# A table built one step earlier, scores on three banks and more filler products in a perceiver block

## The chip, the cores and the metric

The kernel runs on one core of a Trainium2 chip. TensorE (PE) multiplies, VectorE (DVE) and ScalarE (ACT) work elementwise and reduce, GpSimd (POOL) converts and issues some DMAs, SyncE (SP) issues the others. The metric is the device time of one execution in microseconds (us), the median of three runs. TensorE runs at one of two clock levels, 1.2 or 2.4 GHz; the profile gives the granted clock as a share of the higher.

## The reference

Six layers work on the tokens x, 8 x 32 tokens of width 256, each as x = x + f(layernorm(x)):

```python
x = x + L0_xattn(_layernorm(x), ctx)      # self and cross attention, projections rounded to fp8
x = x + L0_attn(_layernorm(x))            # causal conv, state-space scan
x = x + L0_ffn(_layernorm(x))             # 8 experts, the best 2 of each token
x = x + L1_xattn(_layernorm(x), ctx, mask)  # masked read of the contexts
x = x + L1_attn(_layernorm(x))            # rotary attention, 16 heads
x = x + L1_ffn(_layernorm(x))             # weights w = lut[idx], 16 values
```

The first is the longest. For each of 8 contexts of 512 rows it forms keys and values from the context, normalises each key, takes scores of 16 heads, a softmax, and mixes the values:

```python
kvx = einsum('bsi,oi->bso', cond, w_kv_x)
kx, vx = split(kvx, 2, axis=-1)
kx = _ln(kx.reshape(b, sc, g, d), kxln_w, kxln_b)
xout = _gqa(qx, kx, vx.reshape(b, sc, g, d))
core = _gqa(q, k, v)                      # the self attention, "core"
catq = _div_clamp_fp8(concatenate([core, xout]), proj_smooth)
return einsum('bsi,oi->bso', catq, wproj) * (proj_in_scale * proj_w_scale)
```

The last layer's weights are looked up: an index from 0 to 15 for each of 3 x 1536 x 128 elements, and a table of 16 values.

## The kernel before

**Front, to about 130 us.** PE centres a weight (L1511), then makes six projections of the tokens (`project`, L1438) and turns their heads (`turn`, L1456); DVE and ACT normalise the heads between. `cross_queries` (L1465, L1470) folds the keys' weight into the queries, which gives A and beta. The self attention is `scores_core` (L1487), a softmax on DVE and ACT, and `mix_core` (L1504), in two rounds. `z_act` is a semaphore by which DVE waits after each round of heads until ACT has its share done. The array beta is turned by four DVE transposes (L1780) between the two rounds of weights.

**Loop, steps b = 0 to 7, about 130 to 376 us.** Each engine has its own order of work, written out; semaphores join them. In step b PE does the scores of context b (four tiles t, each six products, `product`, L410 to L412), the mixing of context b-1 in two halves (L437) with the turning of the maxima (L420) and the softmax's sum (`total`, L446) between and behind them, the spread of the maxima (L427), in odd steps from 3 on the values of a pair of contexts (L488), and the keys of context b+1 (again L410 to L412, eight half tiles of six products each on banks 0 and 1). ACT splits A (L526), takes the inverse of the sums (L581, L582), splits the next context in two parts (L532), squares the keys with a sum (L543), takes the root (L553, L554) and the exponentials (L576). DVE scales the scores out of the bank (L663) and adds up the sum (L668), takes the maxima (L729 to L731), shifts (L736), normalises (L742 to L749) and makes the keys' scales (L710 to L714). The bank is chosen by

```python
                    if not (isinstance(b, int) and n < 2):
                        pe.wait_ge(scaled, n - 1)
                    product(bank(2 + t % 2), k, t, A_hi, lo).then_inc(st_full, 1)
```

**The table.** lut[idx] is a sum over 8 pairs of table values. For pair k and part m (of three) ACT makes a `leaf` (L618: one of the pair's two values, by the lowest bit of the index), DVE a `term` (L625: the leaf where the rest of the index is 2k, else 0), and a DMA of POOL's queue adds it to the table (L644). The leaf of pair k+1 and part m overwrites the term of pair k, so it waits for that DMA. Step b, from 1 to 6, does pair b-1; pairs 6 and 7 are done during the experts, each added by DVE (L635). The lowest bits are taken by DVE (L784, L785) after step 0.

**Tail, 376 us to the end.** The other five layers follow one another; each begins with a norm in DVE and ACT, after which PE turns h (L945). While PE has nothing to do it issues `keep_clock(n, bank)` (L937), n bf16 products of 128x512 with no use: 12, 14, 14, 14 and 14 of them ahead of the five norms' turning and 28 in the rotary attention.

## Time and profile before

| | us |
|---|---|
| median of 3 runs | 521.88 (520.35 to 522.84) |
| the profiled execution, its time | 520.56 |
| its span, first to last instruction | 518.7 |
| PE busy | 453.6 |
| DVE busy | 362.8 |
| ACT busy | 253.2 |
| mean granted clock | 0.967 |

The span lies 1.9 us below the profiled execution's time. Of the stages the front takes 130 us with PE busy for 103.12, the loop 246 with PE busy for 230.42, the experts (404 to 447) 43 with PE busy for 42.95, and the last three layers (447 to 518) 71 with 57.68. A row of the timeline has its start, its duration, the engine, the line and the operation, and in brackets the idle time ahead of it with what ended that. Neighbouring instructions of one line are put together, with their count after the x.

### The profile page before, as it was taken

The numbers are of one execution on the slowest core, as the hardware profiler recorded it, in microseconds if no ns is written. First come the engines' busy times: TensorE is split into PE (matmuls) and PEld (weight loads), VectorE is DVE, ScalarE is ACT, GpSimd is POOL, SyncE is SP. The second block draws the span as 40 slices with busy tenths as digits, with TensorE's granted clock in tenths as the row PEclk, the third lists the DMA queues.
The fourth block names the chain that finished last, engine by engine and source line by source line (L and its number), as shares of the span: only waits on it lengthen the run. The fifth ranks groups of instructions, "written<-read, shape, count | busy, mean of one in ns | idle before, by whom it ended". The sixth has DMA issues, their size and how long they took to land.

```text
span 518.7 us, 6469 instructions
## 1 busy us (share of the span) xinstructions
PE 453.6 (87%) x2222; PEld 307.4 (59%) x2228; DVE 362.8 (70%) x728; ACT 253.2 (49%) x790; POOL 21.9 (4%) x30
## 2 busy tenths in 40 slices
PE   1969897869999899899989999999667999788787
PEld 0434443457768475658656675657544888436466
DVE  5784848895594868589885888596765699734631
ACT  1366888674462675847766575842002343120110
POOL 0000000004000000100010010100020000000000
PEclk9999999797999999999999999999799999998999
DMA  8163201404100203734646853980039450300000
GB/s 319 54 261 141 81 10 71 163 3 183 42 0 1 81 0 94 140 74 107 155 102 138 286 99 79 186 332 1 0 126 371 145 181 0 112 2 0 1 1 21
DMA packets 13183, 53.98 MB, mean 104 GB/s; under 512 B 1696, under 2 KB 2528, under 8 KB 11616
## 3 DMA queue, kind: packets, MB, share of 16 engines
q1 hardware_dynamic: 10992, 41.80, 22.2%
q0 software_dynamic: 2160, 11.80, 11.6%
q8 instruction: 16, 0.26, 0.2%
q14 instruction: 15, 0.12, 0.1%
HBM read 41.53 MB, written 0.26 MB: 81 GB/s over the span
## 4 chain that ended last, share of the span: by engine, by line
PE 67%; DVE 18%; ACT 10%; issue 4%; DMA 1%; DVEq 0%; ACTq 0%
PE PS L437 11%; PE PS L410 8%; PE PS L412 7%; PE PS L411 7%; PE PS L995 5%; PE PS L488 3%; PE PS L457 3%; PE PS L1470 3%; ACT sq_dt.float L543 2%; PE PS L1104 2%; PE PS L1006 2%; ACT raw_dt.float L1574 2%; DVE small_dt.float L1697 2%; PE PS L1465 1%; PE PS L1055 1%
## 5 line engine op out<-in xcount | busy, mean ns | idle before, releaser
L543 ACT ACTIVATE sq_dt.float<-PS 128x128 bf16<-128x128 f32 x256 | 67.0, 278 | 32.3 <-PE PS L412 29.0
L410 PE MATMUL PS<-wkc_dt.float32r,ctx_hi_dt.float32r 128*128 128x512 f32 x128 | 54.4, 425 | 5.7 <-ACT sq_dt.float L543 5.7
L437 PE MATMUL PS<-s_dt.float,ctx_ring_dt.float 128*128 128x512 f32 x128 | 57.5, 592 | 0.0
L543 ACT ACTIVATION_READ_ACCUMULATOR sq_dt.float<-PS 128x1 f32 x256 | 53.5, 209 | 0.0
L411 PE MATMUL PS<-wkT_dt.float32r,ctx_hi_dt.float32r 128*128 128x512 f32 x128 | 50.8, 397 | 0.0
L412 PE MATMUL PS<-wkc_dt.float32r,ctxT_ring_dt.float32r 128*128 128x512 f32 x128 | 50.8, 397 | 0.0
L1438 PE MATMUL PS<-wch_dt.float,xs_dt.float 128*128 128x512 f32 x96 | 43.9, 613 | 0.0
L618 ACT ACTIVATE luttmp_dt.float<-low_bit_dt.float,vec_dt.float,small_dt.float 128x1536 f32<-128x1536 uint8 x24 | 39.1, 1654 | 0.0
L437 PEld LDWEIGHTS PS<-s_dt.float,ctx_ring_dt.float 128*128 128x128 f32 x128 | 23.6, 190 | 24.0 <-issue 23.5
L625 DVE SCALAR_TENSOR_TENSOR luttmp_dt.float<-idx_dt.float,luttmp_dt.float 128x1536 f32<-128x1536 uint8 x21 | 36.5, 1751 | 0.0
L410 PEld LDWEIGHTS PS<-wkc_dt.float32r,ctx_hi_dt.float32r 128*128 128x128 f32 x128 | 24.4, 190 | 19.3 <-ACT sq_dt.float L543 14.5
L1438 PEld LDWEIGHTS PS<-wch_dt.float,xs_dt.float 128*128 128x128 f32 x96 | 18.7, 197 | 23.3 <-issue 23.3
L284 ACT ACTIVATE small_dt.float<-small_dt.float 128x2 f32<-128x2 f32 (+1 forms) x12 | 3.6, 299 | 55.8 <-DVE small_dt.float L275 51.4
L410 PE MATMUL PS<-A_hi_dt.float32r,ctx_hi_dt.float32r 128*128 128x512 f32 x64 | 25.9, 405 | 4.3 <-DVE s_dt.float L663 4.3
L412 PEld LDWEIGHTS PS<-wkc_dt.float32r,ctxT_ring_dt.float32r 128*128 128x128 f32 x128 | 24.3, 190 | 5.7
L663 DVE TENSOR_TENSOR s_dt.float<-PS,small_dt.float 128x512 f32<-128x512 f32 x32 | 21.5, 689 | 8.3 <-PE PS L412 7.8
L411 PEld LDWEIGHTS PS<-wkT_dt.float32r,ctx_hi_dt.float32r 128*128 128x128 f32 x128 | 24.5, 192 | 3.5
L411 PE MATMUL PS<-A_dt.float32r,ctx_hi_dt.float32r 128*128 128x512 f32 (+1 forms) x64 | 25.0, 390 | 0.0
L412 PE MATMUL PS<-A_hi_dt.float32r,ctxT_ring_dt.float32r 128*128 128x512 f32 x64 | 25.0, 390 | 0.0
L736 DVE TENSOR_TENSOR s_dt.float<-s_dt.float,PS 128x2048 f32<-128x2048 f32 x8 | 18.3, 2287 | 8.9 <-PE PS L427 8.9
L581 ACT ACTIVATE vecs_dt.float<-PS 128x512 f32<-128x512 f32 x8 | 4.8, 597 | 38.3 <-PE PS L446 38.3
L710 DVE TENSOR_SCALAR small_dt.float<-small_dt.float 128x32 f32<-128x32 f32 x8 | 1.5, 184 | 28.9 <-ACT sq_dt.float L543 28.9
(267 smaller groups left out, 888.6 us busy)
## 6 DMA issues: line engine op xcount, KB each, us to landing
lutw_dt.float<-luttmp_dt.float POOLq DMA_DIRECT2D x15, 768.0 KB, 7.2
wch_dt.float<-in_chunks SPq DMA_DIRECT2D x6, 1024.0 KB, 4.8
ctxT_ring_dt.float<-in_ctxT SPq DMA_DIRECT2D x8, 512.0 KB, 3.3
ctx_ring_dt.float<-in_ctx SPq DMA_DIRECT2D x8, 512.0 KB, 4.0
...
luttmp_dt.float<-in_idx SPq DMA_DIRECT2D x3, 768.0 KB, 5.6
...
```

The source lines that it names most:

```text
L410: nc.tensor.matmul(o, x_hi, hi[:, c, :], start=c == 0, stop=False)
L411: nc.tensor.matmul(o, x_hi, lo[:, c, :], start=False, stop=False)
L412: last = nc.tensor.matmul(o, x_lo, hi[:, c, :], start=False, stop=c == CT - 1)
L437: last = nc.tensor.matmul(bank(5 + c), keysr[k][:, t, c * 128:c * 128 + 128], sS[k][:, t, :], start=t == 0, stop=t == KT - 1)
L457: last = nc.tensor.matmul(o[:, j, :], catc[:, i, j * 128:j * 128 + 128], wpc[:, i, :], start=i == 0 and j == 0, stop=i == NH - 1, skip_gro ...
L543: last = nc.scalar.activation(sq[:, (4 * hf + g) * D:(4 * hf + g + 1) * D], bank(hf)[:, g * D:(g + 1) * D], ACT.Square, accum_out=ssq[:, k ...
L618: nc.scalar.activation(lutt[:, m, :], low_bit[:, m, :], ACT.Identity, scale=lut_gap[:, k:k + 1], bias=col("lut", 2 * k)).then_inc(lut_leaf, 1)
L625: nc.vector.scalar_tensor_tensor(lutt[:, m, :] if k else lutw[:, m, :], idx[:, m, :], float(2 * k), lutt[:, m, :], ALU.is_equal, ALU.mult) ...
L663: nc.vector.tensor_tensor(sS[k][:, t, :].rearrange("p (g q) -> p g q", g=G), bank(2 + t % 2, G, 64), krs[:, k, t, :].unsqueeze(2).broadcas ...
L736: nc.vector.tensor_tensor(sS[k], sS[k], bank(4).unsqueeze(1).broadcast_to([128, KT, 512]), ALU.subtract)\
L995: last = nc.tensor.matmul(o[:, m, :], wgu[e % 4][:, i, w0:w0 + 128], hT[:, c, :], start=c == 0, stop=c == CT - 1)
L1438: last = nc.tensor.matmul(bank(q), xs[:, VARIANT[n], c, j * 128:j * 128 + 128], wch[n % 2][:, c, hf * 512:hf * 512 + 512], start=c == 0, s ...
```

## The change

- The table's pairs are one step earlier: step b does pair b, from 0 to 6, and only pair 7 is done during the experts, with its additions by POOL's DMA too (`add_terms`). All three leaves of a step stand ahead of ACT's inverse; two did before. Low bits 0 and 1 are taken ahead of the first key scales, low bits 2 in step 0.
- The scores of steps 1 to 7 use banks 2, 3, 7 and 2 for their four tiles, those of step 0 banks 2 and 3 as before. Bank 7 holds the core's projection until DVE has added it to x; that addition moves from step 1 to the end of step 0, and the third tile of step 1 waits for it.
- beta is turned in step 0 of the loop, ahead of the maxima.
- `scores_core(3)` stands behind `project(5)`, and DVE's wait for z_act comes later, ahead of the root of the next heads.
- Fillers: 14 at the start and 5 after the first turning are new; 12 become 20 (norm 1), 14 become 24 (norm 3), 14 become 18 (norm 4), 28 become 38 (rotary). Those of norms 2 and 5 stay at 14.
- The placing of buffers is another, and `round_fp8` works in place with as many instructions as before.

```diff
+        def score_bank(b, t, *dims):
+            return bank((2, 3, 2, 3)[t] if isinstance(b, int) and b == 0 else (2, 3, 7, 2)[t], *dims)
...
-                    if not (isinstance(b, int) and n < 2):
-                        pe.wait_ge(scaled, n - 1)
+                    if t == 2 and isinstance(b, int) and b == 1:
+                        pe.wait_ge(core_added, 1)
+                    if isinstance(b, int) and b == 0:
+                        if t > 1:
+                            pe.wait_ge(scaled, t - 1)
+                    elif t == 3:
+                        pe.wait_ge(scaled, 4 * b + 1)
...
-                if 1 <= b <= LUT_STEPS:
-                    leaf(act, b - 1, 0)
-                    leaf(act, b - 1, 1)
+                if b <= LUT_STEPS:
+                    for m in range(3):
+                        leaf(act, b, m)
                 if prev:
                     inverse(b - 1)
                 if next_context:
                     split_context(b + 2, k)
-                if 1 <= b <= LUT_STEPS:
-                    leaf(act, b - 1, 2)
...
-        def add_term(dve, k, m):
...
+        def add_terms(pool, k):
+            for m in range(3):
+                pool.wait_ge(lut_term, 3 * k + m + 1)
+                pool.dma_start(lutw[:, m, :], lutt[:, m, :], accum_op=ALU.add).then_inc(lut_added[m], 16)
...
+        def turn_beta():
+            dve.wait_ge(catc_ready, 2)
+            for q in range(4):
+                quadrant = slice(32 * q, 32 * q + 32)
+                last = nc.vector.transpose(betaT[quadrant], beta.rearrange("p (j q) t -> p q j t", q=4)[quadrant, q])
...
-            keep_clock(12, 7)
+            keep_clock(20, 7)
...
-            keep_clock(14, 6)
+            keep_clock(24, 6)
             turn_norm(3, 6)
...
-            keep_clock(14, 6)
+            keep_clock(18, 6)
             turn_norm(4, 6)
...
-            keep_clock(28, 6)
+            keep_clock(38, 6)
...
-            pe.wait_ge(lut_summed, 6)
+            for m in range(3):
+                pe.wait_ge(lut_added[m], 16 * (LUTN // 2 - 1))
...
             pe.wait_ge(ld_const, 32)
+            keep_clock(14, 0)
...
             last.then_inc(ring_full, 4)
+            keep_clock(5, 0)
...
-            scores_core(3)
             project(5)
+            scores_core(3)
...
+                if k:
+                    dve.wait_ge(z_act, k)
                 newton(dve, step, rs[:, 0:NH], rs0[:, 0:NH], var[:, 0:NH], nt[:, 0:NH])
...
-                dve.wait_ge(z_act, k + 1)
```

ACT in a step of the loop with a table pair, before (A_hi: the queries' upper part; luttmp: the leaves; vecs: the sums; sq: the keys' squares):

```order
L526 ACTIVATE A_hi_dt.float32r<-A_dt.float 128x1024 [waits st_full]
L618 ACTIVATE luttmp_dt.float<-low_bit_dt.float,vec_dt.float,small_dt.float 128x1536 [waits lut_term] x2
L581 ACTIVATE vecs_dt.float<-PS 128x512 [waits sum_full]
L582 ACTIVATE vecs_dt.float<-vecs_dt.float 128x512 [waits act_step]
L532 ACTIVATE ctx_hi_dt.float32r<-ctxT_ring_dt.float 128x1024 [waits ld_ctxT0]
L618 ACTIVATE luttmp_dt.float<-low_bit_dt.float,vec_dt.float,small_dt.float 128x1536 [waits lut_term]
L543 ACTIVATE sq_dt.float,small_dt.float<-PS 128x128 [waits sq_ready,kx_full,krs_ready]
```

And after the change:

```order
L536 ACTIVATE A_hi_dt.float32r<-A_dt.float 128x1024 [waits st_full]
L624 ACTIVATE luttmp_dt.float<-low_bit_dt.float,vec_dt.float,small_dt.float 128x1536 [waits lut_added0]
L624 ACTIVATE luttmp_dt.float<-low_bit_dt.float,vec_dt.float,small_dt.float 128x1536 [waits lut_added1]
L624 ACTIVATE luttmp_dt.float<-low_bit_dt.float,vec_dt.float,small_dt.float 128x1536 [waits lut_added2]
L589 ACTIVATE vecs_dt.float<-PS 128x512 [waits sum_full]
L590 ACTIVATE vecs_dt.float<-vecs_dt.float 128x512 [waits act_step]
L542 ACTIVATE ctx_hi_dt.float32r<-ctxT_ring_dt.float 128x1024 [waits ld_ctxT0]
L553 ACTIVATE sq_dt.float,small_dt.float<-PS 128x128 [waits sq_ready,kx_full,krs_ready]
```

The third leaf has moved from between the context's split and the squares to the front of the inverse, and the leaves wait for the DMAs (lut_added).

PE in step 1 of the loop, from the second tile of the scores to the first product of the third, before (PS is the bank, `scaled` counts DVE's scalings):

```order
L410 MATMUL PS<-A_hi_dt.float32r,ctx_hi_dt.float32r 128x512 [waits scaled]
L411 MATMUL PS<-A_dt.float32r,ctx_hi_dt.float32r 128x512
L412 MATMUL PS<-A_hi_dt.float32r,ctxT_ring_dt.float32r 128x512
L410 MATMUL PS<-A_hi_dt.float32r,ctx_hi_dt.float32r 128x512
L411 MATMUL PS<-A_dt.float32r,ctx_hi_dt.float32r 128x512
L412 MATMUL PS<-A_hi_dt.float32r,ctxT_ring_dt.float32r 128x512
L410 MATMUL PS<-A_hi_dt.float32r,ctx_hi_dt.float32r 128x512 [waits scaled]
```

After the change:

```order
L421 MATMUL PS<-A_hi_dt.float32r,ctx_hi_dt.float32r 128x512
L422 MATMUL PS<-A_dt.float32r,ctx_hi_dt.float32r 128x512
L423 MATMUL PS<-A_hi_dt.float32r,ctxT_ring_dt.float32r 128x512
L421 MATMUL PS<-A_hi_dt.float32r,ctx_hi_dt.float32r 128x512
L422 MATMUL PS<-A_dt.float32r,ctx_hi_dt.float32r 128x512
L423 MATMUL PS<-A_hi_dt.float32r,ctxT_ring_dt.float32r 128x512
L421 MATMUL PS<-A_hi_dt.float32r,ctx_hi_dt.float32r 128x512 [waits core_added]
```

The waits for DVE's scaling have gone, and the third tile waits in this step for the core's sum.

DVE in step 0 of the loop, before (L650 makes the lower part of A, L729 takes the maxima, L736 shifts the scores):

```order
L650 TENSOR_TENSOR A_dt.float32r<-A_dt.float,A_hi_dt.float32r 128x1024 [waits A_hi_ready]
L729 TENSOR_REDUCE small_dt.float<-PS 128x4 [waits tr_full]
L730 TENSOR_TENSOR small_dt.float<-small_dt.float 128x4 [waits dve_step]
L731 TENSOR_TENSOR small_dt.float<-small_dt.float 128x4 [waits dve_step]
L736 TENSOR_TENSOR s_dt.float<-s_dt.float,PS 128x2048 [waits mb_full]
L1772 TENSOR_SCALAR qfront_dt.float<-wch_dt.float 128x1024 [waits y_core]
```

After the change:

```order
L650 TENSOR_TENSOR A_dt.float32r<-A_dt.float,A_hi_dt.float32r 128x1024 [waits A_hi_ready]
L714 TENSOR_SCALAR low_bit_dt.float<-idx_dt.float 128x768 [waits idx_ready]
L715 TENSOR_SCALAR idx_dt.float<-idx_dt.float 128x768 [waits dve_step]
L721 STREAM_TRANSPOSE qfront_dt.float<-beta_dt.float 32x1024 [waits catc_ready]
L721 STREAM_TRANSPOSE qfront_dt.float<-beta_dt.float 32x1024 x3
L723 COPY small_dt.float<-qfront_dt.float 128x32 [waits dve_step]
L749 TENSOR_REDUCE small_dt.float<-PS 128x4 [waits tr_full,beta_turned]
L750 TENSOR_TENSOR small_dt.float<-small_dt.float 128x4 [waits dve_step]
L751 TENSOR_TENSOR small_dt.float<-small_dt.float 128x4 [waits dve_step]
L756 TENSOR_TENSOR s_dt.float<-s_dt.float,PS 128x2048 [waits mb_full]
L1786 TENSOR_SCALAR qfront_dt.float<-wch_dt.float 128x1024 [waits y_core]
```

Two operations on the low bits, four transposes of beta and a copy now stand ahead of the maxima.

## Rows read from the trace of the kernel before

**Rows 1.** The page: busy time by engine; the chain that ended last, by engine.
```profile
PE 453.6 (87%) x2222; PEld 307.4 (59%) x2228; DVE 362.8 (70%) x728; ACT 253.2 (49%) x790; POOL 21.9 (4%) x30
...
PE 67%; DVE 18%; ACT 10%; issue 4%; DMA 1%; DVEq 0%; ACTq 0%
```

**Rows 2.** The page's groups: two matmul shapes of the loop, one of the table.
```profile
L410 PE MATMUL PS<-wkc_dt.float32r,ctx_hi_dt.float32r 128*128 128x512 f32 x128 | 54.4, 425 | 5.7 <-ACT sq_dt.float L543 5.7
...
L625 DVE SCALAR_TENSOR_TENSOR luttmp_dt.float<-idx_dt.float,luttmp_dt.float 128x1536 f32<-128x1536 uint8 x21 | 36.5, 1751 | 0.0
...
L410 PE MATMUL PS<-A_hi_dt.float32r,ctx_hi_dt.float32r 128*128 128x512 f32 x64 | 25.9, 405 | 4.3 <-DVE s_dt.float L663 4.3
```

**Rows 3.** Timeline (start, duration, idle before, releaser), PE, steps 1 and 2.
```profile
193.58 0.50 PE L410 MATMUL PS<-A_hi_dt.float32r,ctx_hi_dt.float32r 128*128 128x512 f32 x1 [0.59 <-DVE s_dt.float L663]
...
196.44 3.59 PE L437 MATMUL PS<-s_dt.float,ctx_ring_dt.float 128*128 128x512 f32 x8
...
207.58 0.39 PE L412 MATMUL PS<-wkc_dt.float32r,ctxT_ring_dt.float32r 128*128 128x512 f32 x1
...
209.64 0.50 PE L410 MATMUL PS<-wkc_dt.float32r,ctx_hi_dt.float32r 128*128 128x512 f32 x1 [1.67 <-ACT sq_dt.float L543]
```

**Rows 4.** Timeline, ACT, step 2.
```profile
204.80 0.60 ACT L581 ACTIVATE vecs_dt.float<-PS 128x512 f32<-128x512 f32 x1 [3.99 <-PE PS L446]
...
206.92 1.65 ACT L618 ACTIVATE luttmp_dt.float<-low_bit_dt.float,vec_dt.float,small_dt.float 128x1536 f32<-128x1536 uint8 x1
```

**Rows 5.** The page's DMA issues: the table's accumulating transfers.
```profile
lutw_dt.float<-luttmp_dt.float POOLq DMA_DIRECT2D x15, 768.0 KB, 7.2
```

**Rows 6.** Timeline, DVE, step 0 of the loop.
```profile
130.23 0.18 DVE L710 TENSOR_SCALAR small_dt.float<-small_dt.float 128x32 f32<-128x32 f32 x1 [6.12 <-ACT sq_dt.float L543]
...
142.74 0.69 DVE L729 TENSOR_REDUCE small_dt.float<-PS 128x4 f32<-128x512 f32 x1 [4.63 <-PE PS L420]
...
157.22 0.18 DVE L710 TENSOR_SCALAR small_dt.float<-small_dt.float 128x32 f32<-128x32 f32 x1 [1.67 <-ACT sq_dt.float L543]
...
164.40 0.69 DVE L663 TENSOR_TENSOR s_dt.float<-PS,small_dt.float 128x512 f32<-128x512 f32 x1 [3.73 <-PE PS L412]
```

**Rows 7.** Timeline, DVE, PE and POOL, before the loop.
```profile
104.66 4.94 DVE L1780 STREAM_TRANSPOSE qfront_dt.float<-beta_dt.float 32x1024 f32<-32x1024 f32 x4
...
105.00 2.01 PE L1504 MATMUL PS<-attn_dt.float,v_dt.float 32*128 32x64 f32 x64
...
115.10 3.69 PE L1504 MATMUL PS<-attn_dt.float,v_dt.float 32*128 32x64 f32 x64 [4.11 <-DVE attn_dt.float L1766]
...
122.99 5.39 POOL L640 CAST idx_dt.float<-luttmp_dt.float 128x1536 uint8<-128x1536 int32 x3 [122.15 <-DMA luttmp_dt.float<-in_idx]
```

**Rows 8.** Windows: us, busy PE, PEld, DVE, ACT, POOL; granted clock, DMA share, GB/s.
```profile
116.00:120.00 4.00, 4.00 (x58) 3.69 (x56) 3.86 (x6) 0.00 (x0) 0.00 (x0) 0.50 0.10 19
```

**Rows 9.** Windows in the tail: experts, masked read, rotary attention.
```profile
404.00:447.00 43.00, 42.95 (x200) 37.12 (x201) 38.48 (x64) 16.87 (x17) 0.00 (x0) 1.00 0.29 99
...
452.00:456.00 4.00, 3.46 (x20) 0.98 (x24) 0.68 (x2) 0.00 (x0) 0.00 (x0) 0.63 0.36 138
...
492.00:496.00 4.00, 3.95 (x15) 2.81 (x15) 0.87 (x2) 0.00 (x0) 0.00 (x0) 0.75 0.00 0
```

**Rows 10.** Timeline, PE, masked read and rotary projections.
```profile
451.10 0.66 PE L945 MATMUL PS<-consts_dt.float,h_dt.float 128*128 128x128 f32 x4 [2.46 <-DVE h_dt.float L290]
...
452.54 5.34 PE L1027 MATMUL PS<-keysT_dt.float,hT_dt.float 128*32 128x512 f32 x32 [0.78 <-DVE hT_dt.float L1300]
...
470.09 7.12 PE L1055 MATMUL PS<-hT_dt.float,rot_dt.float 128*128 128x256 f32 x24 [0.78 <-DVE hT_dt.float L1316]
```

**Rows 11.** Timeline, PE, from the start.
```profile
9.87 1.08 PE L1426 MATMUL PS<-consts_dt.float,raw_dt.float 128*128 128x128 f32 x4 [9.87 <-DVE raw_dt.float L290]
12.13 5.65 PE L1511 MATMUL PS<-raw_dt.float,consts_dt.float 128*128 128x512 f32 x8 [1.18 <-DVE lnT_dt.float L1661]
```

**Rows 12.** Window of one plain step.
```profile
196.44:224.68 28.24, 25.97 (x100) 17.30 (x99) 20.42 (x27) 19.17 (x74) 2.77 (x3) 1.00 0.55 122
```

132 lines of the change are left out of this document (60 added, 72 removed).

## The prediction

> **What bounds the kernel now.** I read the shares of busy time first, then the chain that ended last, the groups of instructions with their idle time, and last the timeline of single stretches. TensorE (PE) is busy for 87% of the span and makes up 67% of the chain; VectorE (DVE) has 18% of the chain and ScalarE (ACT) 10% [rows 1]. So the time is PE's own work, 453.6 us, plus 65.1 us in which PE has nothing to do; and some of that work is slower than it need be, where the granted clock is low. The change takes no work from PE; it can only shorten gaps and slow stretches, and I go through them.
>
> The groups give two gaps inside the loop: 5.7 us ahead of the keys' products, until ACT's squares (L543) have read a bank, and 4.3 us ahead of the scores' products, until DVE's scaling (L663) has [rows 2]. The timeline shows each once: two products 2.06 us apart that elsewhere follow each other every 0.23, with 1.67 idle, and one with 0.59 idle ahead of it [rows 3]. The first stands in steps 1, 2 and 4 with 1.67 each and in step 6 with 0.73, the second once in step 0 and once in each of steps 2 to 7.
>
> **Table and key stalls.** In a step ACT does leaves 0 and 1, waits 3.99 us for the sums, takes the inverse, splits the context, does leaf 2 (1.65) and only then squares the keys that PE has long had ready [rows 4]. After the change all three leaves stand ahead of the inverse. The third fills 1.65 of those 3.99 us, so the inverse is not later, and the squares start 1.6 earlier. The stall goes whole, with about 0.1 of restart: 3 x 1.75 + 0.75 = 6.0; I take 5.9. Steps 3 and 5 have the values' matmuls in that place and no stall to give. Next late would be the squares' own pace, 0.25 us apiece, eight in 2.0 against the 2.8 of PE's tile: nothing.
>
> From pair 2 on the leaves wait for the accumulating DMA of the pair before. Behind a late leaf stand the inverse, the split and the squares, and PE waits for these. The DMAs land in 7.2 us median [rows 5]. The last term of a step is issued about 12 us before the leaf that needs it in a plain step and about 9 in one with values, and ACT keeps 2.3 us of idle time behind. I count nothing, and keep it as the rival on the slower side.
>
> **Three banks and score stalls.** With two banks tile 2 waits for the scaling of tile 0 or 1, with three only tile 3 waits. A tile costs PE 1.38 us (six products at 0.23); the stall and the slow restart (a product of 0.50 instead of 0.39 [rows 3]) are 0.86 at most, six times, 5.1. It could come to nothing, if DVE's scaling is what the next stage waits for; but 3.4 us of mixing stand on PE between the last scores tile and the maxima, and DVE has its last tile done 1.7 us into it, so I take 5.1. Bank 7 is free once DVE has added the core's sum, now at the end of step 0, where DVE is idle for 3.73 us [rows 6]. Loop together 11.0 less, bounds 0 and 12.
>
> **Step 0.** Turning beta takes 4.94 us and its copy 0.2 [rows 7]; with low_bits(2), 0.7, it comes into the 4.63 us in which DVE waits for the maxima [rows 6]. That is 5.8 into 4.63: the maxima are 1.2 late, and PE, which waits for their spread, with them: +1.2. The three terms of pair 0 (1.75 each, 5.25 [rows 2]) come before the key scales, against idle stretches of 1.67 and 3.73 us and 2.1 us of low bits that left: 5.25 into 7.5 fits. Low bits 0 and 1 (1.4) stand in 6.12 idle us [rows 6]; two of POOL's three casts, 5.39 us from 122.99 on [rows 7], come first, so they are done by 128 of the old time, 2 us early.
>
> **Front.** Between two rounds of weights DVE turns beta, and PE sits 4.11 us until mix_core(4) at 115.10 [rows 7]. Without the turning the second round starts as soon as PE has its scores (108.05, DVE began at 109.74): 1.4 or so. The wait z_act that goes was 1.1 us of DVE idle time in the same chain, and project(5) ahead of scores_core(3) gives PE something to do in a gap of 3.9 us before: 0.6 that reaches DVE. Together 3.1; bounds 1.4 and 6.0 (4.94 and 1.1).
>
> In that stretch the granted clock falls to 0.50, the lower of the two levels [rows 8], after the 4.11 us without work. mix_core(4) took 3.69 there against 2.01 for its like before [rows 7], and the first key tiles lose 1.8: if the clock stays up, 3.4. The gap is still some 2.7, and a gap of 2.46 in the tail was followed by 0.63 [rows 9, 10]. This is even: I take 1.7.
>
> At the start PE's first work is at 9.87, and then come eight products in 5.65 us, 0.71 apart, where such products take 0.43 at full clock [rows 11]. Fourteen fillers run ahead of that while PE is idle, five more between. Eight at 0.43 are 3.4, so 2.2 at best; below, five fillers of 0.22 to 0.43 could stand in the way of the products by 1.5, beyond the 1.18 idle there. I take -1.6, bounds +1.5 and -2.2.
>
> **Tail.** The last pair moves off DVE: six terms and six sums of 1.75 become three terms. PE is busy 42.95 of 43 us there [rows 9]: nothing. What is left is fillers. Ahead of the masked read PE ends 14 of them at 448.6, waits 2.46 us and then does 32 products in 5.34 at clock 0.63 [rows 9, 10]. 24 at 0.22 end near 450.9, when h is nearly there: 2.0 (1.1 to 2.1 by the clock, the rest of DVE's chain). Ahead of the rotary projections 18 shrink the gap; 24 products took 7.12 [rows 10], at 0.22 each they would take 5.3: 1.8. Within rotary attention 38 end 0.55 after the weights, but hold the clock that was 0.75 at 492 [rows 9], worth 2.0: 1.4. After the ssm's norm 0.6. All of it 5.8; I take 4.4, bounds +1 and -5.8.
>
> The Trainium skill ("TensorE: Matmul & The Clock Gate", Part 1: The HAM clock gate) says that the throttled clock is the default, that recent activity releases it, and that what is looked at runs free of the program, so that the change comes elsewhere from run to run. By that rule no filler's gain and no gap's loss is a fixed number. These terms, up to 10.8 in all, would then come out anywhere between none and all, and differently in two runs of one kernel; no row here can show that, with one trace.
>
> **Sum.** -1.6 - 3.1 - 1.7 + 1.2 - 11.0 - 4.4 = -20.6. On the profiled execution's 520.56 that is 500.0. The median of the runs is 521.88, 1.3 above it, so 501.3 for a median; I give 501.
>
> **Rivals.** B: the clock doesn't answer to fillers. Then the start, the front's clock and 4.2 of the tail are missing, 7.5: 508.8. For it: gaps of 2.5 to 2.7 remain in places. Against it: 14 fillers were followed by a full clock wherever the gap behind them was under 0.9.
> C: the loop's stalls only move. Each comes back as a wait for the spread or the key scales, since DVE has the same work in a shorter step. Against it: DVE is busy 20.4 of 28.2 us, PE 26.0 [rows 12]. It would leave 1 of 11: 511.
> D, the slower side: the inverse behind a leaf that waits for its DMA. From a landing of 11 us in a step with values and 14 in a plain one on, ACT's spare 2.3 is used up; at 18 us each of the five steps whose leaves wait for a DMA (2 to 6) would lose about 5 us, half of it reaching PE's path: 501 + 11 (the loop's gain gone) + 5 x 5 x 0.5 = 524.5. For it: the transfers run at another place of the step, beside the context loads. Against it: none of the 15 took over 8.3.
>
> **Chances.** As forecast 0.62 (own range 495 to 506), B 0.19, C 0.13, D 0.03, the rest mixtures of small terms. A measurement of this kernel tells 0.5% apart, 2.6 us. Faster by more 0.94, within it 0.03, slower 0.03. The range, 494 to 511, leaves out D, half of C and the case that each term comes out at its best bound.
>
> **What would show it.** In the new trace: no idle time ahead of the keys' products in steps 1, 2 and 4, and none at the third scores tile from step 1 on; plain steps of 25.6 us instead of 28.2, steps with values 29.2 instead of 30.1; ACT's wait for the sums 2.3 instead of 4.0; the maxima of step 0 about 1.2 later than PE's chain; clock 1.00 in the masked read (32 products in 3.4 to 4.3), in the rotary projections (24 in 5.3) and in the output products. It is wrong if ACT stands idle before a leaf, if a plain step stays above 27.5, or if the windows behind the fillers are still at 0.6.

## The result and the profile after

The changed kernel takes 504.64 us (median of 4 executions, 503.81 to 508.3) against 522.36 for the kernel before (4 executions, 520.35 to 526.61). The ratio is 0.9691, with a 95% interval of 0.9639 to 0.9743. The forecast was 501 with a range of 494 to 511: faster, as forecast, by 16 us (by the ratio) to 18 us (by the medians) where 20.6 were worked out.

The profiled execution took 508.3 us, span 506.5, and is the slowest of the four; the other three have a mean clock of 0.973, this one 0.966. Here are the page's shares and chain after the change, which answer to [rows 1], and the two groups that answer to [rows 2]:

```profile
PE 462.1 (91%) x2273; PEld 311.5 (62%) x2279; DVE 356.4 (70%) x722; ACT 253.7 (50%) x790; POOL 27.8 (5%) x36
...
PE 74%; DVE 14%; ACT 9%; issue 2%; DMA 1%; SPq 0%; DVEq 0%; ACTq 0%
...
L421 PE MATMUL PS<-wkc_dt.float32r,ctx_hi_dt.float32r 128*128 128x512 f32 x128 | 55.0, 429 | 0.4
...
L421 PE MATMUL PS<-A_hi_dt.float32r,ctx_hi_dt.float32r 128*128 128x512 f32 x64 | 25.2, 394 | 2.2 <-DVE s_dt.float L663 2.2
```

PE's idle time ahead of the keys' products went from 5.7 to 0.4 us and that ahead of the scores' from 4.3 to 2.2, of which 2.15 stand in step 0. ACT's idle time ahead of the inverse, 3.99 in [rows 4], is now 2.43 in each of the steps 1 to 6; here is step 2:

```profile
195.38 4.77 ACT L624 ACTIVATE luttmp_dt.float<-low_bit_dt.float,vec_dt.float,small_dt.float 128x1536 f32<-128x1536 uint8 x3
202.58 0.60 ACT L589 ACTIVATE vecs_dt.float<-PS 128x512 f32<-128x512 f32 x1 [2.43 <-PE PS L457]
```

In each step from 0 to 6 the three leaves run without idle time ahead of them or between them (4.77 or 4.78 us for three), so none of them waited for its DMA (6.8 us median to landing). The stages, each from a start in one trace to the same start in the other:

| stretch | before, us | after, us | difference |
|---|---|---|---|
| start to the mixing of context 0 (L437/L448) | 168.21 | 168.43 | +0.22 |
| to the mixing of context 7 | 188.15 | 177.17 | -10.98 |
| to the ssm's first products (L956/L966) | 31.43 | 30.17 | -1.26 |
| to the router (L982/L992) | 15.23 | 18.13 | +2.90 |
| to the masked read (L1027/L1037) | 49.52 | 49.00 | -0.52 |
| to the rotary projections (L1055/L1065) | 17.55 | 17.89 | +0.34 |
| to the last layer (L1104/L1115) | 30.25 | 27.29 | -2.96 |
| to the end | 18.36 | 18.42 | +0.06 |

So the loop gave what was worked out, 11.0 us, and all the rest together 1.2 of the 9.6 expected. That is between two single traces, and the one after is the slowest of its four: by the medians and the ratio all the rest gave 5 to 7 us. The front begins well. PE's first rows, which answer to [rows 11]:

```profile
5.12 5.32 PE L363 MATMUL PS<-consts_dt.float 128*128 128x512 bf16 x14 [5.12 <-DMA consts_dt.float<-in_consts]
10.28 0.60 PE L1438 MATMUL PS<-consts_dt.float,raw_dt.float 128*128 128x128 f32 x4
10.72 1.24 PE L363 MATMUL PS<-consts_dt.float 128*128 128x512 bf16 x5
12.06 3.67 PE L1524 MATMUL PS<-raw_dt.float,consts_dt.float 128*128 128x512 f32 x8
15.71 14.00 PE L1451 MATMUL PS<-wch_dt.float,xs_dt.float 128*128 128x512 f32 x32
```

The eight products take 3.67 instead of 5.65 and the projections start at 15.71 instead of 17.62, 1.9 earlier. Most of it is gone at 36 us, where eight products that took 3.70 before take 5.40, behind the same idle time. Before, and after:

```profile
37.85 3.70 PE L1465 MATMUL PS<-zu_dt.float,small_dt.float 128*128 128x512 f32 x8 [2.96 <-ACT zu_dt.float L1585]
```

```profile
36.06 5.40 PE L1478 MATMUL PS<-zu_dt.float,small_dt.float 128*128 128x512 f32 x8 [2.97 <-ACT zu_dt.float L1598]
```

Then the second place, PE between 95 and 116 us, which answers to the PE rows of [rows 7]:

```profile
95.27 1.10 PE L1500 MATMUL PS<-zu_dt.float,kT_dt.float 128*32 128x64 f32 x64
100.38 2.90 PE L1469 MATMUL PS<-consts_dt.float,raw_dt.float 128*128 128x128 f32 x16 [4.01 <-ACT v_dt.float L1566]
103.21 3.69 PE L1517 MATMUL PS<-attn_dt.float,v_dt.float 32*128 32x64 f32 x64
106.83 1.94 PE L1500 MATMUL PS<-xs_dt.float,kT_dt.float 128*32 128x64 f32 x64
...
114.19 2.01 PE L1517 MATMUL PS<-attn_dt.float,v_dt.float 32*128 32x64 f32 x64 [1.01 <-DVE attn_dt.float L1780]
```

The gap of 4.11 us ahead of mix_core(4) has shrunk to 1.01, and mix_core(4) takes 2.01 again. But it starts only 0.9 us earlier (114.19, 115.10 before): most of the gap has closed because PE comes to it later, not because DVE is done earlier. With scores_core(3) behind project(5), a gap of 4.01 us stands ahead of the last turning, and now the turning (2.90, 1.91 before), mix_core(3) (3.69, 2.01 before) and the scores behind it (1.94, 1.10 before) are at the lower clock. Before, the gap stood two pieces of work earlier, and these were slow:

```profile
92.53 1.94 PE L1487 MATMUL PS<-zu_dt.float,kT_dt.float 128*32 128x64 f32 x64 [3.92 <-ACT zu_dt.float L1585]
94.40 8.93 PE L1438 MATMUL PS<-wch_dt.float,xs_dt.float 128*128 128x512 f32 x16
```

They take 1.10 and 7.03 after the change. The windows, which answer to [rows 8 and 9] with the same columns, show it, with two more stretches:

```profile
100.00:104.00 4.00, 3.62 (x32) 3.07 (x32) 2.38 (x5) 4.00 (x8) 0.00 (x0) 0.70 0.72 307
104.00:108.00 4.00, 4.00 (x100) 3.88 (x100) 0.00 (x0) 1.68 (x4) 0.00 (x0) 0.50 0.01 4
...
144.00:148.00 4.00, 4.00 (x15) 2.98 (x14) 3.90 (x5) 1.54 (x11) 0.00 (x0) 0.75 0.00 0
...
384.00:388.00 4.00, 3.78 (x12) 2.64 (x13) 0.48 (x1) 0.00 (x0) 0.00 (x0) 0.50 1.05 398
```

Before, the clock was full at 140 to 148 and in the ssm's last products (its first twelve were slow, 4.46 us instead of 2.78 after). The stretches that the tail's fillers aimed at came out as expected, which answers to [rows 10]; between them stands the reading of the contexts' values, at the lower clock:

```profile
442.90 3.64 PE L1037 MATMUL PS<-keysT_dt.float,hT_dt.float 128*32 128x512 f32 x32 [0.78 <-DVE hT_dt.float L1311]
...
449.95 5.24 PE L1051 MATMUL PS<-keys_dt.float,probs_dt.float 128*32 128x256 f32 x64
...
460.79 5.45 PE L1065 MATMUL PS<-hT_dt.float,rot_dt.float 128*128 128x256 f32 x24 [0.78 <-DVE hT_dt.float L1327]
...
479.08 3.72 PE L1100 MATMUL PS<-rot_dt.float,probs_dt.float 128*128 128x256 f32 x16 [0.98 <-DVE probs_dt.float L1133]
```

The 32 products take 3.64 instead of 5.34, the 24 take 5.45 instead of 7.12 and the 16 take 3.72 instead of 5.41. The low clock has gone to the ssm's last products and to 448 to 456 instead, where the 64 products took 3.66 before.

### The profile page after: what moved, and what is told of

Same layout as the page of the kernel before. It is cut to its first block, busy times and chain, and to the rows that moved or that the text cites. A ratio compares the mean times of both kernels' runs of the same rounds, so it can differ in the third digit from the quotient of the medians.

```text
span 506.5 us, 6549 instructions
## 1 busy us (share of the span) xinstructions
PE 462.1 (91%) x2273; PEld 311.5 (62%) x2279; DVE 356.4 (70%) x722; ACT 253.7 (50%) x790; POOL 27.8 (5%) x36
## 4 chain that ended last, share of the span: by engine, by line
PE 74%; DVE 14%; ACT 9%; issue 2%; DMA 1%; SPq 0%; DVEq 0%; ACTq 0%
PE PS L448 11%; PE PS L421 8%; PE PS L423 8%; PE PS L422 8%; PE PS L363 6%; PE PS L1005 5%; PE PS L498 3%; PE PS L1016 3%; PE PS L1483 3%; ACT raw_dt.float L1587 2%; PE PS L1115 2%; PE PS L1478 2%; ACT raw_dt.float L1566 2%; ACT zu_dt.float L1598 2%; PE PS L1451 1%
## 5 line engine op out<-in xcount | busy, mean ns | idle before, releaser
L448 PE MATMUL PS<-s_dt.float,ctx_ring_dt.float 128*128 128x512 f32 x128 | 57.5, 592 | 0.0
L1451 PE MATMUL PS<-wch_dt.float,xs_dt.float 128*128 128x512 f32 x96 | 42.1, 593 | 0.0
L363 PE MATMUL PS<-consts_dt.float 128*128 128x512 bf16 x141 | 35.9, 414 | 5.8 <-DMA consts_dt.float<-in_consts 5.1
L448 PEld LDWEIGHTS PS<-s_dt.float,ctx_ring_dt.float 128*128 128x128 f32 x128 | 23.6, 190 | 24.0 <-issue 23.5
L637 POOL DMA_DIRECT2D lutw_dt.float<-luttmp_dt.float x21 | 18.2, 869 | 223.8 <-DVE luttmp_dt.float L631 223.8
L363 PEld LDWEIGHTS PS<-consts_dt.float 128*128 128x128 bf16 x147 | 15.2, 106 | 24.8 <-issue 6.3
```

Source lines behind the costliest of these rows:

```text
L363: nc.tensor.matmul(bank(nb), busy[:, 0:128], busy, start=True, stop=True)
L448: last = nc.tensor.matmul(bank(5 + c), keysr[k][:, t, c * 128:c * 128 + 128], sS[k][:, t, :], start=t == 0, stop=t == KT - 1)
L637: pool.dma_start(lutw[:, m, :], lutt[:, m, :], accum_op=ALU.add).then_inc(lut_added[m], 16)
L1451: last = nc.tensor.matmul(bank(q), xs[:, VARIANT[n], c, j * 128:j * 128 + 128], wch[n % 2][:, c, hf * 512:hf * 512 + 512], start=c == 0, s ...
```

## The experiments

Each group ran beside the kernel before on one chip; ratios are to it, with 95% intervals. The theory: the loop's gain is the two stalls and fixed, the rest hangs on where PE is idle and so on the clock. A ratio can differ from the quotient of the two medians by some tenths of a per cent.

**a_again**, the changed kernel once more, without an edit.

> The changed kernel once more, to see how much two executions of one program differ. Theory T (the loop's gain is fixed, the clock's is not): the mixing of context 1 to 7 starts 25.8, 25.8, 29.1, 25.8, 29.1 and 25.5 us apart again within 0.2, and the stretches at the lower clock (in the first trace 36 to 44, 100 to 112, 140 to 148, 380 to 392 and 448 to 456 us) lie elsewhere or are missing; median 502 to 506. Rival F (the low stretches are fixed by the program's gaps): the same stretches again, each within one 4 us slice, and the profiled execution again near 508.

504.93 us (502.44 to 509.93, 6 executions), ratio 0.9693 (0.9627 to 0.9759). The mixing starts at 170.04, 195.82, 221.59, 250.71, 276.48, 305.59 and 331.18: steps of 25.8, 25.8, 29.1, 25.8, 29.1 and 25.6, as in the first trace of this kernel. The low stretches are the same ones (36 to 44, 96 to 116, 144, 356 to 364, 380 to 396, 448 to 456), with other borders and lengths. Both sides were partly right: where the clock falls is set by the gaps, how much of the work behind each gap is slow is not. Six executions of one program had mean clocks of 0.963 to 0.980, and those at 0.963 took 509.6 and 509.9, the one at 0.980 took 502.4.

**b_leaf**, the kernel before with one edit:

```diff
                     leaf(act, b - 1, 1)
+                    leaf(act, b - 1, 2)
                 if prev:
                     inverse(b - 1)
                 if next_context:
                     split_context(b + 2, k)
-                if 1 <= b <= LUT_STEPS:
-                    leaf(act, b - 1, 2)
```

> The kernel before, with only the third leaf moved ahead of ACT's inverse; the pairs stay where they were. Theory T: the idle time of PE ahead of the keys' products (5.7 us) goes, three plain steps are 1.75 us shorter each and the last with a table 0.75; the whole 5 to 6 us below before (ratio 0.989). Rival M (a stall only moves): PE's idle time comes back at the spread or the scores, steps stay at 28.2, ratio 0.998 or more.

515.84 us beside 522.08, ratio 0.9884 (0.9816 to 0.9951): a gain clear of the noise, as expected. The group of the keys' products, and that of the scores', which keeps its stall:

```profile
L410 PE MATMUL PS<-wkc_dt.float32r,ctx_hi_dt.float32r 128*128 128x512 f32 x128 | 54.2, 423 | 0.4
...
L410 PE MATMUL PS<-A_hi_dt.float32r,ctx_hi_dt.float32r 128*128 128x512 f32 x64 | 26.0, 406 | 4.3 <-DVE s_dt.float L662 4.3
```

5.7 us of idle time became 0.4. From the mixing of context 0 to that of context 6 it is 166.64 us instead of 172.15, 5.5 less. The stall goes, and it comes back in none of the other waits of the loop.

**b_banks**, the kernel before with the scores on three banks and the core's sum at the end of step 0:

```diff
-                    if not (isinstance(b, int) and n < 2):
-                        pe.wait_ge(scaled, n - 1)
+                    if t == 2 and isinstance(b, int) and b == 1:
+                        pe.wait_ge(core_added, 1)
+                    if isinstance(b, int) and b == 0:
+                        if t > 1:
+                            pe.wait_ge(scaled, t - 1)
+                    elif t == 3:
+                        pe.wait_ge(scaled, 4 * b + 1)
...
-                    product(bank(2 + t % 2), k, t, A_hi, lo).then_inc(st_full, 1)
+                    product(score_bank(b, t), k, t, A_hi, lo).then_inc(st_full, 1)
```

> The kernel before, with only the scores of steps 1 to 7 on three banks and the core's sum at the end of step 0. Theory T: PE's idle time ahead of the scores' products falls from 4.3 us (7 times) to 0.6 (step 0), the six steps are 0.8 shorter each, 5 us in all, ratio 0.990. Rival M: DVE's scaling ends no earlier, the maxima are waited for, gain under 1.5 us.

516.09 us beside 522.08, ratio 0.9909 (0.9868 to 0.9949), 12 executions. Its two groups, the other way round:

```profile
L419 PE MATMUL PS<-wkc_dt.float32r,ctx_hi_dt.float32r 128*128 128x512 f32 x128 | 54.4, 425 | 5.8 <-ACT sq_dt.float L552 5.8
...
L419 PE MATMUL PS<-A_hi_dt.float32r,ctx_hi_dt.float32r 128*128 128x512 f32 x64 | 25.2, 394 | 0.6 <-DVE s_dt.float L672 0.6
```

The same stretch is 166.67 us, 5.5 less. 5.5 and 5.5 make 11.0, and the changed kernel needs 161.17 for it, 11.0 less: the two edits add up. They leave nothing for the table's pairs being one step earlier, which was not run alone; in the loop it shows no gain.

**b_fill**, the kernel before with the change's fillers alone:

```diff
+            keep_clock(14, 0)
...
+            keep_clock(5, 0)
...
-            keep_clock(12, 7)
+            keep_clock(20, 7)
```

and 24, 18 and 38 as in the change.

> The kernel before, with only the fillers of the change (14 and 5 at the start, 20, 24, 18 and 38 in the tail). If the clock answers to them as forecast: 1.6 at the start and 4.4 in the tail, 6 in all, ratio 0.989. If what the fillers win in one place is lost in the next stretch after a gap (the first trace of the changed kernel has 5.40 us for eight products at 36 us, where before had 3.70): 1 to 2.5 us, ratio 0.995 to 0.998.

517.53 us beside 522.08, ratio 0.9948 (0.9905 to 0.999), so 2.7 us by the ratio, with an interval of 0.5 to 5.0. In its trace, from the masked read on, the clock is full until 512 us, and the mean is 0.977 (0.967 in the first trace of before). At 36 to 40 us it is 0.65, where the kernel before had 1.00. So the second case: a part of what the fillers win goes in the next stretch behind a gap.

**a_oldfill**, the changed kernel with the fillers of before (the reverse edit).

> The changed kernel with the fillers of before (none at the start, 12, 14, 14 and 28 in the tail). By the forecast's terms 1.6 + 4.4 = 6.0 us more: 511, ratio 0.980. By what the fillers alone gave the kernel before (0.9948, 2.7 us): 507 to 508, ratio 0.974.

508.36 us beside 521.28, ratio 0.9748 (0.9695 to 0.9801), 3.4 us above the changed kernel's 504.93 by medians, 2.9 by ratios; the intervals of the two ratios overlap. From either side the fillers are worth some 3 us, half of the 6.0 in the sum. The two agree, and neither is sharp by itself.

**a_front**, the changed kernel with the order in front as before:

```diff
+            scores_core(3)
             project(5)
-            scores_core(3)
...
-                if k:
-                    dve.wait_ge(z_act, k)
...
+                dve.wait_ge(z_act, k + 1)
```

> The changed kernel with scores_core(3) ahead of project(5) again and DVE's wait for z_act back behind each round of heads. By the forecast the core's chain gets 1.7 us longer of the 3.1 (1.1 of z_act and 0.6 of the order), with the clock stretch that hangs on it up to 3.4: 506 to 508, ratio to before 0.972 to 0.976. Rival: the two edits only move PE's gap (4.01 us ahead of turn(4) instead of 3.92 ahead of scores_core(3) and 4.11 ahead of mix_core(4)), so the loop starts within 0.5 us of where it does now, ratio 0.969.

504.19 us, ratio 0.9693 (0.9637 to 0.9749), the same as the changed kernel: the rival. In its trace PE is idle for 3.92 us ahead of scores_core(3) again, project(5) takes 8.95 us, the gap ahead of mix_core(4) is 2.45 us, mix_core(4) starts at 113.66 (114.19 in the changed kernel) and the mixing of context 0 at 167.87 (168.43). The order and z_act were put back together, so neither has a price of its own.

**a_beta**, the changed kernel with beta turned between the two rounds of weights, as before the change:

```diff
             core_weights(0)
+            for q in range(4):
+                quadrant = slice(32 * q, 32 * q + 32)
+                last = nc.vector.transpose(betaT[quadrant], beta.rearrange("p (j q) t -> p q j t", q=4)[quadrant, q])
+            step(last)
...
-                    turn_beta()
```

> The changed kernel with beta turned between the two rounds of weights again, where DVE now stands idle 6.35 us, and not in step 0. If the turning in step 0 costs what was forecast, the maxima of step 0 come 1.2 us earlier, PE's idle time ahead of the spread falls from 2.37 to about 1.2, and the front loses nothing or up to 1.4: 503.5 to 505, ratio 0.967 to 0.970. Rival: the second round of weights is late by the 4.9 us again, mix_core(4) waits 4 us, and the clock with it: 506 to 508.

501.23 us (500.89 to 502.66), ratio 0.9625 (0.9575 to 0.9676), below what was expected. The interval overlaps with the changed kernel's, but the slowest of these five executions is faster than nine of the changed kernel's ten, of which the quickest took 502.44. The front and step 0 of its trace:

```profile
113.12 2.01 PE L1515 MATMUL PS<-attn_dt.float,v_dt.float 32*128 32x64 f32 x64 [2.49 <-DVE attn_dt.float L1778]
...
128.84 0.50 PE L421 MATMUL PS<-A_hi_dt.float32r,ctx_hi_dt.float32r 128*128 128x512 f32 x1 [0.63 <-DVE s_dt.float L663]
...
140.39 0.65 PE L438 MATMUL PS<-consts_dt.float,small_dt.float 128*128 128x128 f32 x4 [1.18 <-DVE small_dt.float L749]
...
152.30 7.07 PE L468 MATMUL PS<-zu_dt.float,catc_dt.float 128*128 128x256 f32 x32
```

The last three of these rows in the changed kernel, where mix_core(4) starts at 114.19:

```profile
129.82 0.50 PE L421 MATMUL PS<-A_hi_dt.float32r,ctx_hi_dt.float32r 128*128 128x512 f32 x1 [2.15 <-DVE s_dt.float L663]
...
142.55 1.11 PE L438 MATMUL PS<-consts_dt.float,small_dt.float 128*128 128x128 f32 x4 [2.37 <-DVE small_dt.float L751]
...
156.07 7.07 PE L468 MATMUL PS<-zu_dt.float,catc_dt.float 128*128 128x256 f32 x32
```

With the turning in step 0 PE is idle for 2.37 us ahead of the spread instead of 1.18, as forecast. Not forecast is what follows: from the spread to the core's second half it is 13.52 us instead of 11.91, at a clock of 0.82 and 0.75 (full in the trace of a_beta). The other traces agree: the gap ahead of the spread is 2.37 in the changed kernel, a_again, a_front and a_oldfill, and behind it the clock is low in all four; it is 1.18 or 1.19 in the kernel before, b_leaf, b_banks, b_fill, a_beta and a_beta_front, and behind it the clock is full in all six. The turning in front cost nothing, since DVE stood idle there for 6.35 us in the changed kernel. The third scores tile starts 1.0 us earlier here too, at 128.84, since mix_core(4) was 1.1 earlier. That part is not the turning's but the clock's: it was 0.83 at 104 to 108 and full at 108 to 112, where the changed kernel had 0.50 and 0.52.

**a_beta_front**, both of the last two edits together.

> The changed kernel with beta turned in front again and also scores_core(3) ahead of project(5) and the wait for z_act as before: the front of the kernel before, with the start's fillers, and the loop and tail of the changed one. If the order and z_act are worth something where the turning isn't in step 0 (DVE then has the turning behind the first weights, and PE 4.1 us idle before mix_core(4) as before), mix_core(4) is 1.1 to 1.7 later and the clock behind it falls again: 504 to 506, ratio 0.969, against 0.9625 with beta in front alone. If they are worth nothing, as with beta in step 0 (ratio 0.9693 for both): 501 to 502, ratio 0.963.

505.92 us beside 520.92, ratio 0.9709 (0.9671 to 0.9747). The gap ahead of mix_core(4) is 4.10 us again and mix_core(4) takes 3.69. The four cases:

| | beta turned in front | beta turned in step 0 |
|---|---|---|
| order and z_act as before | 505.92, 0.9709 | 504.19, 0.9693 |
| order and z_act as changed | 501.23, 0.9625 | 504.93, 0.9693 |

By the medians the order and z_act alone gain 4.7 us, the turning's move alone 1.7, and both together leave 1.0; with the order changed, the move of the turning costs 3.7: it is the one part of the change found to cost time. The four were not all run on one chip. The ratios, which allow for that, give 4.4 for the order, 0.8 for the turning's move, 0.8 for both and 3.5 for the move with the order changed. The intervals overlap in each pair. Of the executions, all five of a_beta are below all six of a_beta_front (from 504.89) and below nine of the changed kernel's ten; a difference of 0.8 is within the noise.

**a_gaps**, the changed kernel with fillers in the gaps that the trace shows ahead of low clock:

```diff
+                if n == 0:
+                    pe.wait_ge(proj_read, 5)
+                    keep_clock(12, 0)
                 pe.wait_ge(ring_read["act"], reads("act", RING_AT[f"turn{n}"] + 4))
...
             scores_core(3)
+            keep_clock(18, 4 + RING_AT["mix3"] % 4)
             turn(4)
...
+            keep_clock(8, 5)
             spread(0)
...
             mix(7, 1, 1)
+            keep_clock(16, 1)
             values(3, 0)
```

and 5 and 8 in the ssm, ahead of the waits for conv_ready and diag_d.

> The changed kernel with more fillers in the gaps behind which the trace shows the lower clock: 12 ahead of the first cross_queries (2.97 us idle), 18 ahead of turn(4) (4.01), 8 ahead of step 0's spread (2.37), 16 ahead of the last values (4.09), 5 and 8 in the ssm (1.25 and 1.96). If idle time is what lowers the clock there, the low windows at 36, 100 to 112, 144, 356 and 380 to 392 go, mean clock 0.98 or more, and the time falls by 6 to 9 us: 496 to 499, ratio 0.953 to 0.957. If fillers only stand in the way: no change or up to 2 us slower, 504 to 507.

498.81 us (498.6 to 502.53), ratio 0.9603 (0.9547 to 0.9659). The profiled execution has a mean clock of 0.997, and the windows of the former low stretches:

```profile
100.00:112.00 12.00, 9.48 (x216) 7.82 (x214) 7.61 (x13) 10.28 (x33) 0.00 (x0) 1.00 0.14 57
140.00:148.00 8.00, 8.00 (x37) 6.12 (x37) 7.29 (x7) 4.83 (x35) 0.00 (x0) 1.00 0.00 0
380.00:392.00 12.00, 10.39 (x54) 7.64 (x55) 7.22 (x32) 2.58 (x5) 0.00 (x0) 1.00 0.42 159
```

PE's idle time is what lowers its clock there, and work without use keeps it up. The time fell by 6.1 us by the medians (504.93 to 498.81), the lower end of what was expected, and by 4.7 by the ratios, which is less than expected. In step 0 the idle time ahead of the third scores tile stayed at 2.19, and behind it stands the one low stretch that is left in this trace:

```profile
125.67 0.50 PE L421 MATMUL PS<-A_hi_dt.float32r,ctx_hi_dt.float32r 128*128 128x512 f32 x1 [2.19 <-DVE s_dt.float L665]
```

```profile
124.00:128.00 4.00, 2.33 (x7) 1.93 (x8) 2.76 (x8) 1.67 (x6) 0.00 (x0) 0.81 0.00 0
```

The profiled execution is the quickest of the five; the others took up to 502.53, at mean clocks down to 0.986.

**g_late**, a_gaps with POOL's casts held back and all low bits in step 0:

```diff
                 pool.wait_ge(ld_idx[m], 16)
+                pool.wait_ge(krs_ready, 1)
...
-                    low_bits(2)
+                    for m in range(3):
+                        low_bits(m)
...
-            low_bits(0)
-            low_bits(1)
             key_scale(0, 0)
```

> The kernel with fillers in the gaps, with POOL's three casts held back until the key scales of step 0 are written (a wait on krs_ready), and all low bits in step 0 ahead of beta's turning. If it is the casts that stretch DVE's operations, then before the scales L305, L798 (the two small ones) and L656 take 1.23, 0.17 and 1.22 us again, the scaling of step 0 starts on time (idle ahead of the third tile 0.6 instead of 2.19), and operations with two SBUF inputs beside the casts in step 0 (L670, 0.69 otherwise) are stretched instead, up to 1.9 each; low bits 0 and 1 and the later casts put the maxima 1.4 to 3 us back, so the whole is the same as or up to 3 us above the kernel with fillers in the gaps (499 to 502). If the stretching is of another cause (the index loads' DMA), L305 and L656 stay at 2.5.

502.06 us (497.94 to 502.32), ratio 0.9602 (0.9543 to 0.966): by the ratio the same as a_gaps. On DVE's operations the casts act as expected. DVE and POOL in a_gaps, beside the casts:

```profile
116.25 2.49 DVE L305 TENSOR_TENSOR catc_dt.float<-catc_dt.float,qfront_dt.float 128x1024 f32<-128x1024 f32 x1
118.67 1.42 DVE L798 TENSOR_TENSOR small_dt.float<-vec_dt.float 128x8 f32<-128x8 f32 x1
...
120.32 2.47 DVE L656 TENSOR_TENSOR ctxT_ring_dt.float32r<-ctxT_ring_dt.float,ctx_hi_dt.float32r 128x1024 fp32r<-128x1024 f32 x1
```

```profile
116.20 1.46 POOL L644 CAST idx_dt.float<-luttmp_dt.float 128x1536 uint8<-128x1536 int32 x1 [115.36 <-DMA luttmp_dt.float<-in_idx]
118.16 1.91 POOL L644 CAST idx_dt.float<-luttmp_dt.float 128x1536 uint8<-128x1536 int32 x1 [0.50 <-DMA luttmp_dt.float<-in_idx]
120.25 1.47 POOL L644 CAST idx_dt.float<-luttmp_dt.float 128x1536 uint8<-128x1536 int32 x1 [0.18 <-DMA luttmp_dt.float<-in_idx]
```

The same DVE operations in g_late, where the casts run from 124.97 on:

```profile
116.22 1.23 DVE L305 TENSOR_TENSOR catc_dt.float<-catc_dt.float,qfront_dt.float 128x1024 f32<-128x1024 f32 x1
117.37 0.16 DVE L800 TENSOR_TENSOR small_dt.float<-vec_dt.float 128x8 f32<-128x8 f32 x1
...
117.77 1.23 DVE L657 TENSOR_TENSOR ctxT_ring_dt.float32r<-ctxT_ring_dt.float,ctx_hi_dt.float32r 128x1024 fp32r<-128x1024 f32 x1
```

Each of the three casts put some 1.25 us on a DVE operation. The index loads' DMA ran in both, so it is not the cause. Once POOL runs later, other operations are beside the casts: of three operations with two SBUF inputs (L671, 0.69 otherwise) one took 1.11, the others 0.79 and 0.75, less than the 1.9 that was allowed for.

```profile
129.61 1.11 DVE L671 TENSOR_TENSOR vecs_dt.float<-vecs_dt.float,s_dt.float 128x512 f32<-128x512 f32 x1
```

The stall in step 0 reads 0.60 in this trace instead of 2.19, but PE gained nothing by that: the third scores tile starts at 125.61, where it started at 125.67.

```profile
125.61 0.50 PE L421 MATMUL PS<-A_hi_dt.float32r,ctx_hi_dt.float32r 128*128 128x512 f32 x1 [0.60 <-DVE s_dt.float L666]
```

PE came to it later, since the clock was 0.57 at 112 to 116 (1.00 in a_gaps) and eight key products behind mix_core(4) took 0.63 instead of 0.39. What the two edits give where the clock is full shows in g_final, below. The spread then waits for 4.1 us behind all the low bits and the turning, 1.67 of them filled, and the mixing of context 0 starts at 164.43 (164.18 in a_gaps).

This kernel's executions have two levels, 498 us at a mean clock of 0.997 (two of six) and 502 at 0.990 (four). The profiled one is at 502, and the difference from a_gaps' 498.6 lies in the ssm and the experts: the ssm's first twelve products take 4.46 us instead of 2.78, and the experts' first 32 take 8.68 instead of 7.15, behind the same fillers and the same idle times.

```profile
371.38 4.46 PE L968 MATMUL PS<-hpad_dt.float,ssmw_dt.float 128*64 128x256 f32 x12 [0.94 <-DVE hpad_dt.float L1221]
```

**g_beta**, a_gaps with beta in front, all low bits in step 0 and 4 fillers ahead of the spread.

> The kernel with fillers in the gaps (first of them as before, 4 ahead of step 0's spread), with beta turned in front again and all low bits taken in step 0 instead of two ahead of the first key scales. Turning beta 5.13 us in DVE's 3.38 idle us delays mix_core(4) by 1.8; the first scaling of step 0 is no longer late (1.6 less idle ahead of the third scores tile), the maxima are 1.2 earlier: 1.0 below the kernel with fillers in the gaps, ratio to before 0.958. Rival: DVE's operations that run beside POOL's casts (L796 1.42 us instead of 0.17, L654 2.48 instead of 1.22) still hold the first scaling back, and the 1.8 stays: 499 to 500.5, ratio 0.962.

502.39 us (499.96 to 502.97), ratio 0.9631 (0.9579 to 0.9684), above the 0.958 that was expected and the rival's 0.962, and no better than a_beta. The gap ahead of mix_core(4) is 3.92 us, mix_core(4) starts 1.4 later than in a_gaps, and the clock at 112 to 120 is 0.55 and 0.60. So where PE comes early, DVE's turning in front does delay it. By the spread this is made up for, since the turning no longer stands in step 0: the mixing of context 0 starts at 164.53, 0.35 later than in a_gaps and 0.1 later than in g_late. The rest of the profiled time is the level of 502 again, with the same slow stretches in the ssm and the experts as in g_late.

**g_final**, g_late with 10 fillers ahead of mix_core(4), 24 ahead of norm 1 and 4 and 3 behind the turnings of norms 1 and 2.

> The kernel with fillers in the gaps and POOL's casts held back, with more of them: 10 ahead of mix_core(4) (2.46 us idle, behind which the clock was 0.57), 24 instead of 20 ahead of norm 1 and 4 behind its turning, 3 behind norm 2's turning. Its two levels of time (498 at a mean clock of 0.997, 502 at 0.990) should become one: 497 to 498.5 in nearly all executions, ratio to before 0.955. If the fillers behind the turning stand in the way, or the gaps left still let the clock fall, the two levels stay: median 501 to 502, ratio 0.960.

499.9 us (498.93 to 500.6) beside 520.92, ratio 0.9589 (0.9554 to 0.9624), six executions with mean clocks of 0.993 or 0.997. The two levels have come together, to about 1 us apart where they were 4, but even the lower is 1.4 us above that of g_late, so the median is above the 497 to 498.5 expected. At full clock from 88 to 128 us, the third scores tile starts 1.65 us earlier than in a_gaps, with the idle time of the kernel before:

```profile
124.02 0.50 PE L421 MATMUL PS<-A_hi_dt.float32r,ctx_hi_dt.float32r 128*128 128x512 f32 x1 [0.58 <-DVE s_dt.float L667]
```

That is what the held casts and the moved low bits are worth together at that point; which of the two gives it was not told apart. The spread is lost again behind 2.41 us without work (clock 0.81 and 0.76 at 136 to 144; in g_late, behind 2.43, it was full), and the mixing of context 0 starts at 164.39. By the ratio it is the quickest, though its interval overlaps with those of a_gaps and g_late, and a_gaps has the lower median; against the changed kernel's 0.9691 it is faster by 1% of the kernel's time.

## Why the prediction was right, and where it was off

The direction and the loop's mechanism were right. Of the 20.6 us, 11.0 were the loop and came in full; 6.0 were fillers and gave some 3; 3.6 were the front with step 0 and gave about 1. These make 15, against the 16 to 18 measured. Of the forecast's own signs, the plain steps (25.8 us, 25.6 forecast), the steps with values (29.1, 29.2), ACT's wait (2.43, 2.3) and the maxima of step 0 (1.2 later) came; a clock of 1.00 behind the fillers came in the three places named, but not at 36 us (0.60) and 448 (0.72).

**Key stalls and score stalls: right.** 5.9 and 5.1 were forecast, 5.5 and 5.5 measured alone, 11.0 together. Each term was off by 0.4, one up and one down; that the sum is right to the tenth is luck. The leaf fits into ACT's wait for the sums (3.99 to 2.43), and no leaf waited for a DMA: rival D did not appear. Rival C is excluded by both single edits. PE's experts take the same time in both traces (41.7 us from the first product to the last), as forecast.

**Tail: the rows right, the sum off.** Masked read, rotary projections and output products took 3.64, 5.45 and 3.72, each as forecast or within 0.2. But the tail from the ssm's first products on is 0.2 shorter in the profiled execution, where 4.4 were counted for the whole tail, since the ssm's last products fell to 0.50 and the reading of the values at 448 to 0.72 (5.24 us instead of 3.66). Over all executions the fillers gave 3 us of the 6.0 in the sum. The step that failed is the adding up: each filler term was taken as the work behind it at the high clock, with nothing lost elsewhere. Rival B had 1.6 and 4.2 of it missing and came about halfway true.

**Front and step 0: the least of it came.** 3.1 for the chain and 1.7 for the clock were counted against 1.2 for step 0, net 3.6. Measured is the step from a_beta_front to the changed kernel, about 1 us (505.92 to 504.93; ratios 0.9709 to 0.9693), and the first trace has the loop's first mixing 0.2 later, where 5.2 earlier was worked out, the start's fillers included. Four things were missed:

1. project(5) ahead of scores_core(3) was credited with filling PE's 3.9 us. It only moved them: the last turning waits for ACT to read project(5), 4.01 us, and the clock fell there instead. The chain in front was 0.9 us earlier at mix_core(4), not 3.1. The forecast let DVE's second round start when PE had its scores at the full clock of before, 108.05; at the lower clock they came at 108.77.
2. The low bits were "2 us early" in the old times, and counted at nothing. They weren't early: POOL's casts came 2.3 us earlier (120.69, 122.99 before), and DVE's operations beside them were stretched (L796 1.42 us for 0.17, L797 1.37 for 0.16, L714 1.62 for 0.35), and DVE went from the low bits to the key scales (128.19) without idle time, where it had waited 6.12 before. The first scaling was the last to be ready, and PE's idle time ahead of the third scores tile went from 0.60 to 2.15, 1.55 more. In a_front and a_beta, where PE comes later, it is 0.59 and 0.63 and DVE's work the same.
3. Turning beta in step 0 was put at 1.2, which is what the wait shows (1.19 to 2.37). The clock behind that wait was not counted: 1.6 more. The rows of before for the two waits:

```profile
132.34 0.50 PE L410 MATMUL PS<-A_hi_dt.float32r,ctx_hi_dt.float32r 128*128 128x512 f32 x1 [0.60 <-DVE s_dt.float L663]
...
143.89 0.65 PE L427 MATMUL PS<-consts_dt.float,small_dt.float 128*128 128x128 f32 x4 [1.19 <-DVE small_dt.float L731]
```

4. In the start's own term, the fillers gave 1.9 at the first projections, more than the 1.6 in the sum, and 1.7 of it went at 36 us.

The gap ahead of mix_core(4) was to be some 2.7 and was 1.01, because PE came late; where PE's clock is full, in a_gaps, it is 2.44, as forecast. The clock behind it was full, for which 1.7 of 3.4 had been counted, an even chance. a_beta, without the turning's move, took 501.2: that this is the forecast's figure is a coincidence, since the forecast's sum has the move in it.

**The clock rule.** The Trainium skill ("TensorE: Matmul & The Clock Gate", Part 1: The HAM clock gate) was weighed for its sentence that what is looked at runs free of the program. The runs agree with it: six executions of one program had mean clocks of 0.963 to 0.980 and times 7.5 us apart, and the borders of the low stretches differ between two traces. So do single places: behind the same idle times of 0.76 and 1.39 us the 64 products that read the values took 5.24 in the changed kernel and 3.66 in g_late. The runs add that most of the places are the program's own.

**What stays open.** Why g_final's lower level is 1.4 us above g_late's: its trace is of an execution at 0.993, with the clock low at 136 to 144 (0.81, 0.76) and 440 to 448 (0.78, 0.79), and fillers standing in the way weren't told apart from it. The last pair's move to POOL's DMA, the table's earlier pairs and the other placing of buffers were not run alone.
